# Moving 72 edge-row scatters from the first convolution into the recurrent blocks of a fused graph network

## The chip, the cores and the metric

One core of a Trainium2 chip runs the whole program. The metric is the time of one execution on the device in microseconds; smaller is better. The core has TensorE (matmuls; PE in the profile), VectorE (DVE), ScalarE (ACT), GpSimd (POOL) and SyncE (SP), which here only issues DMAs. "PEq" or "SPq" in a row is the instruction queue of that engine.

## The reference

Four graph networks follow one another on 3125 nodes of 128 features, with 100,000 edges (padded to 782 columns of 128 edges), each followed by a residual sum and a normalisation:

```python
x = _layernorm(x + _L0_gnn_ref(...))   # two convolutions: h = x + segment_sum(x[src], dst); two dense layers
x = _layernorm(x + _L1_gnn_ref(...))   # two attention layers
x = _layernorm(x + _L2_gnn_ref(...))   # four recurrent blocks: neighbour sum, dense, gates
x = _layernorm(x + _L3_gnn_ref(x, edge_attr_64, src, dst, ...))
# the last: W = silu(edge_attr @ W1 + b1) @ W2 + b2; msgs = h[dst] * W; sum of msgs by src; two dense layers
```

The last network sums its messages by source node, while the edges arrive ordered by destination. Its input rows, one of 66 floats for each edge (64 attributes and the two node numbers), must therefore be brought into another order.

## The kernel before

The nodes are padded to 3200 and held as 25 tiles of 128. Sums over neighbours in the two convolutions (`gin_conv`, tags g0 and g1) and the recurrent blocks (`gru_block`) are dense matmuls with a 3200 x 3200 matrix of edge counts: `sum_neighbours` (L370) runs 25 tiles times 3 bf16 parts of the features for each half of a group of 5 tiles (GT), and 5 groups (NG) make a layer.

The program is a chain of blocks, each with one program for each engine, and each ends in a barrier of all engines; what runs on two engines in one block is joined there. The order is: constants, `edge_order` (computes the slot of every edge in the new order), `build_counts`, `gin_conv` g0 (the first convolution) and g1, `edge_tables`, two `attention` layers, `softmax_norm`, four times `gru_block`, `edge_messages`, `node_update`.

The edge rows reach their new order by scatters that GpSimd issues beside other work. One scatter writes 128 rows of 264 bytes from SBUF to the table `sorted` in device memory, at the slots that `edge_order` found. There are 782 of them, one for each column of edges, and only `edge_messages` reads `sorted`. The class `Sender` (L1722) does them in batches: `begin` loads the slots of its share and the rows of the first batch; `send` waits for the batch's rows, copies its slots to an index tile (L1749), issues the scatters one by one (L1756), and halfway issues the load of the next batch's rows into the other of two buffers (L1737), after the scatters that read that buffer are done; `end` waits until all scatters have landed. Its core:

```python
        for u in range(self.size):
            if u == self.size // 2:
                if not first:
                    pool.wait_ge(self.sent[1 - s], j * full + s * full)
                self.load(pool, n + 1, 1 - s)
            pool.indirect_dma_start(out=self.D["sorted"], in_=self.held[s][:, u, :], in_offset=None,
                                    out_offset=...).then_inc(self.sent[s], 16)
```

How many go where is set by constants (L1593 to L1596), each a triple of first column, scatters in a batch and number of batches: 168 in `build_counts`, 150 in the first convolution, 32 in `edge_tables`, 108 in each of the four recurrent blocks. In `gin_conv` and `gru_block` GpSimd does nothing else. SyncE loads the features, in g0 also writes the count matrix to memory for the recurrent blocks (L439, 20 MB), and stores each group's result (L446, L1487). In `gin_conv` a group goes from the sums (L370) over a copy by VectorE (L504) and two dense layers (L463, L471) with ScalarE (L483) to VectorE (L510, L514) and the store; in `gru_block` over two dense layers (L1504, L1508), the gates on ScalarE and VectorE, five transposes (L1512) and copies (L1572) to the store. The rows named L420 and L1469 are the places where those blocks are opened and closed.

Of the kernel before, what the change touches and what calls it, by code (L numbers as in the profile page):

```python
# [14 lines left out]
NT = -(-N_NODES // P)  # L15
# [524 lines left out]
def edge_tables(nc, K, D):  # L540
# [5 lines left out]
    with ExitStack() as ctx:  # L546
# [19 lines left out]
        bound = m.sb("p_bound", [1, NT + 1])  # L566
        sender = Sender(m, D, "p", *TABLE_SENDS)
        boundi = m.sb("p_boundi", [1, NT + 1], I32)
# [873 lines left out]
def gru_block(nc, K, D, AT, b, source, from_scale, to_scale, parts, target, residual):  # L1442

    with ExitStack() as ctx:
# [11 lines left out]
        split = Split(m, source, 1, parts, [work[:, i, :].rearrange("p (t c) -> p t c", c=P) for i in range(3)], from_scale)  # L1456
        sender = Sender(m, D, "r", *GRU_SENDS[b])
        y = m.sb("r_y", [P, GT, P])
# [132 lines left out]
NEAR_STEPS = 4  # L1591
ROWW = RBF + 2
COUNT_SENDS = (0, 7, NT - 1)  # L1593
GIN_SENDS = (7 * (NT - 1), 15, 10)
TABLE_SENDS = (7 * (NT - 1) + 150, 16, 2)
GRU_SENDS = [(7 * (NT - 1) + 182 + 108 * b, 9, 12) for b in range(4)]  # L1596
NSC = 7 * (NT - 1) + 182 + 432
SROWS = (NGRP + 1) * EGRP
FILL = (NGRP + 1) * SUB // 11
# [445 lines left out]
def gnn_program(nc, D):  # L2045
# [27 lines left out]
    with ExitStack() as ctx:  # L2073
# [6 lines left out]
        with ExitStack() as ctx2:  # L2080
            AT = Mem(nc, ctx2).sb("gin_counts", [P, NT, NP], BF16)
            build_counts(nc, K, D, AT)
            gin_conv(nc, K, D, AT, "g0", D["x"], 1, D["L0_W1a"], D["L0_b1a"], D["L0_W2a"], D["L0_b2a"], 2 * P,
                     D["gin1"], None, sends=GIN_SENDS, keep=D["kept"])
            gin_conv(nc, K, D, AT, "g1", D["gin1"], 2, D["L0_W1b"], D["L0_b1b"], D["L0_W2b"], D["L0_b2b"], P,
# [95 lines left out]
```

## Time and profile before

| | |
|---|---|
| median of 3 runs | 6274.49 us |
| lowest and highest | 6272.12, 6283.94 us |
| span of the profiled execution | 6282.4 us |
| TensorE busy, share of the span | 4259.3 us, 68% |
| VectorE | 3797.3 us, 60% |
| GpSimd | 3528.6 us, 56% |
| first convolution, start to start of the next block | 966.8 to 1227.4 us |
| four recurrent blocks | 4365.2 to 5093.1 us |

Times in a row are in microseconds from the start of the span. Only one execution is profiled, and its rows are exact for that one alone. A stage that ends in a barrier is as long as its slowest engine, whatever the shares of the span say; so one looks for what each engine waited for at the stage's end. A wait at a barrier is put down to the queue that released it, which is the one that passes the barrier on and not always the one that was late.

### The profile page before, as it was taken

The numbers are of one execution on the slowest core, as the hardware profiler recorded it, in microseconds if no ns is written. First come the engines' busy times: TensorE is split into PE (matmuls) and PEld (weight loads), VectorE is DVE, ScalarE is ACT, GpSimd is POOL, SyncE is SP. The second block draws the span as 40 slices with busy tenths as digits, with TensorE's granted clock in tenths as the row PEclk, the third lists the DMA queues.
The fourth block names the chain that finished last, engine by engine and source line by source line (L and its number), as shares of the span: only waits on it lengthen the run. The fifth ranks groups of instructions, "written<-read, shape, count | busy, mean of one in ns | idle before, by whom it ended". The sixth has DMA issues, their size and how long they took to land. (4 is left out here: it accounts for less than half of the span.)

```text
span 6282.4 us, 102133 instructions
## 1 busy us (share of the span) xinstructions
PE 4259.3 (68%) x26578; PEld 2971.7 (47%) x26579; DVE 3797.3 (60%) x8630; ACT 1047.3 (17%) x1871; POOL 3528.6 (56%) x3626
## 2 busy tenths in 40 slices
PE   3666667395267777776256666666787777788884
PEld 1111115263156565655245555554454555566663
DVE  8777772154589999998456666666211235555553
ACT  0111111102211111111211111111211222222221
POOL 1222224502377777774277777771666667777771
PEclk9999999697589999998567777777898888988885
DMA  4000004201244444442333233334212222222233
GB/s 197 15 12 15 15 12 187 70 15 36 71 128 119 124 118 125 117 126 79 129 82 81 75 82 81 81 76 155 60 55 63 70 71 78 78 78 77 78 78 40
DMA packets 331742, 510.88 MB, mean 81 GB/s; under 512 B 104053, under 2 KB 245407, under 8 KB 321686
## 3 DMA queue, kind: packets, MB, share of 16 engines
q0 software_dynamic: 129376, 287.12, 17.6%
q1 hardware_dynamic: 202166, 221.78, 10.9%
q14 instruction: 158, 1.29, 0.1%
q8 instruction: 42, 0.69, 0.0%
HBM read 406.76 MB, written 101.86 MB: 81 GB/s over the span
## 5 line engine op out<-in xcount | busy, mean ns | idle before, releaser
L1061 POOL DMA_INDIRECT e_ring<-att_rows,e_near x1760 | 1791.3, 1018 | 553.7 <-issue 473.8
L1130 PE MATMUL e_psum<-e_ring,e_whole_pick 128*128 128x264 f32 (+1 forms) x3520 | 840.6, 392 | 244.5 <-DVE e_ring L1295 238.7
L1839 POOL DMA_INDIRECT e_nodes<-x,e_edges x832 | 808.6, 972 | 266.3 <-issue 239.2
L1130 PEld LDWEIGHTS e_psum<-e_ring,e_whole_pick 128*128 128x128 f32 x3520 | 643.6, 227 | 369.5 <-issue 175.8
L1085 PE MATMUL e_px<-t_parts,e_pick 128*128 x5280 | 671.9, 268 | 102.0 <-DVE e_pick L1193 51.5
L1209 DVE TENSOR_TENSOR e_prod<-e_px,e_ring 128x512 f32<-128x512 f32 x660 | 449.9, 682 | 386.8 <-DMA e_ring<-att_rows,e_near 277.4
L285 PE MATMUL b_acc<-b_pick_key,b_pick_lo 128*128 128x416 bf16 (+1 forms) x1960 | 495.9, 341 | 169.9 <-DVE b_pick_key L256 151.6
L1756 POOL DMA_INDIRECT sorted<-rx_held,rx_index x432 | 425.1, 984 | 220.4 <-issue 209.4
L1085 PEld LDWEIGHTS e_px<-t_parts,e_pick 128*128 128x128 bf16 x5280 | 442.8, 107 | 188.7 <-issue 119.2
L1173 ACT ACTIVATE e_whole_pick<-e_pturn 128x512 f32<-128x512 bf16 x440 | 261.7, 595 | 1351.6 <-PE e_pturn L1121 1329.0
L256 DVE TENSOR_SCALAR b_pick_key<-b_lane,b_base,b_keyf 128x800 bf16<-128x800 int16 x980 | 477.1, 487 | 0.0
L1199 DVE TENSOR_REDUCE e_dots<-e_prod 128x8 f32<-128x512 f32 (+1 forms) x660 | 444.8, 674 | 0.0
L1295 DVE TENSOR_TENSOR e_ring<-e_ring 128x1024 f32<-128x1024 f32 (+1 forms) x440 | 416.1, 946 | 26.7 <-issue 26.7
L1876 PE MATMUL e_pa<-e_msg,e_pick 128*128 128x128 f32 x1672 | 296.4, 332 | 191.5 <-DVEq L1938 191.2
L1876 PEld LDWEIGHTS e_pa<-e_msg,e_pick 128*128 128x128 f32 x1672 | 248.6, 228 | 362.7 <-DVEq L1938 355.2
L255 DVE TENSOR_SCALAR b_pick_lo<-b_lane,b_lof 128x128 bf16<-128x128 int16 x980 | 255.7, 261 | 236.8 <-PE b_acc L285 192.7
L370 PE MATMUL g_pa<-gin_counts,g_parts 128*128 x2250 | 312.7, 302 | 120.4 <-DMA g_b<-in_L_b2b 101.9
L285 PEld LDWEIGHTS b_acc<-b_pick_key,b_pick_lo 128*128 128x128 bf16 x1960 | 120.2, 97 | 529.9 <-DVE b_pick_key L256 514.9
L1946 DVE TENSOR_TENSOR agg<-agg,e_pa 128x128 f32 x418 | 120.5, 288 | 381.6 <-PE e_pa L1876 234.5
L209 POOL TENSOR_TENSOR gin_counts<-gin_counts,identb 128x128 bf16 (+1 forms) x25 | 12.7, 507 | 568.9 <-ACT gin_counts L266 568.9
L1089 PE MATMUL e_pside<-t_side,e_pick 128*128 x1760 | 332.1, 189 | 0.0
L370 PEld LDWEIGHTS g_pa<-gin_counts,g_parts 128*128 128x128 bf16 x2250 | 221.1, 99 | 211.9 <-issue 123.5
(348 smaller groups left out, 6766.7 us busy)
## 6 DMA issues: line engine op xcount, KB each, us to landing
e_relb<-place SPq DMA_DIRECT2D x56, 1024.0 KB, 6.0
e_ring<-att_rows,e_near POOLq DMA_INDIRECT x1760, 2.6
sorted<-o_fill SPq DMA_DIRECT2D x11, 2508.0 KB
e_edges<-sorted SPq DMA_DIRECT2D x209, 132.0 KB
kept<-gin_counts SPq DMA_DIRECT2D x5, 4000.0 KB
rx_held<-in_edge_rows POOLq DMA_DIRECT2D x52, 297.0 KB
e_nodes<-x,e_edges POOLq DMA_INDIRECT x832
gru_late<-kept SPq DMA_DIRECT2D x3, 4000.0 KB, 32.6
```

Of the source, the lines that this page charges most:

```text
L256: dve.tensor_scalar(pick_key[:, b, :], lane[:, :], base[:, ds(w, 1)], keyf[:, ds(c, 1)], ALU.add, ALU.is_equal).then_inc(picked, 1)
L285: mm = pe.matmul(acc[q % 2][:, h, 0:z - a], pick_lo[:, b, :], pick_key[:, b, a:z], start=False, stop=False, skip_group_check=True)
L370: mm = pe.matmul(banks, parts[:, k, j, f * P:(f + 1) * P], AT[:, j, ds(g * GW + half * HW, HW)], start=(j == 0 and k == 0), stop=(j == NT ...
L1061: pool.indirect_dma_start(out=ring[:, s, r, 0:wd + HEADS], out_offset=None, in_=xrows, in_offset=bass.IndirectOffsetOnAxis(ap=near[:, s, r ...
L1085: mm = pe.matmul(px[g % 2][:, x * wd:(x + 1) * wd], pick[:, 1 - s, r, :], parts[:, n, ds(t, 1), :].rearrange("p o c -> p (o c)"), start=(n ...
L1130: mm = pe.matmul(psum[q % 2][:, 0:RING], whole_pick[:, q % 2, c, :], ring[:, s, q * G + c, :], start=(c == 0), stop=(c == G - 1))
L1199: dve.tensor_reduce(dots[:, s, :, g * XB:(g + 1) * XB].rearrange("p h x -> p x h"), prod[:, g % 4, :].rearrange("p (x h c) -> p x h c", x= ...
L1209: dve.tensor_tensor(prod[:, g % 4, :].rearrange("p (x c) -> p x c", x=XB), px[g % 2][:, :].rearrange("p (x c) -> p x c", x=XB), ring[:, 1 ...
L1295: dve.tensor_tensor(rows_, rows_, ring[:, s, q * G:(q + 1) * G, wd:wd + HEADS].unsqueeze(3).broadcast_to([P, G, HEADS, ch]), ALU.mult).the ...
L1756: pool.indirect_dma_start(out=self.D["sorted"], in_=self.held[s][:, u, :], in_offset=None, out_offset=bass.IndirectOffsetOnAxis(ap=self.in ...
L1839: pool.indirect_dma_start(out=nodes[:, q, u, :], out_offset=None, in_=source, in_offset=bass.IndirectOffsetOnAxis(ap=edges[:, q, u, RBF + ...
L1876: mm = pe.matmul(pa[s][:, part * P:(part + 1) * P], pick[:, s, u, :], msg[:, s, u, :], start=(u % (SUB // HALVES) == 0), stop=(u % (SUB // ...
```

## The change

Only the constants that divide the scatters change. The first convolution issues 6 batches of 13, 78 in all, instead of 10 of 15. The edge tables keep their 2 batches of 16 and take the columns that follow. Each of the four recurrent blocks issues 14 batches of 9, 126 in all, instead of 12 of 9. The same 782 columns are scattered, each once.

```diff
 COUNT_SENDS = (0, 7, NT - 1)
-GIN_SENDS = (7 * (NT - 1), 15, 10)
-TABLE_SENDS = (7 * (NT - 1) + 150, 16, 2)
-GRU_SENDS = [(7 * (NT - 1) + 182 + 108 * b, 9, 12) for b in range(4)]
+GIN_SENDS = (7 * (NT - 1), 13, 6)
+TABLE_SENDS = (7 * (NT - 1) + 78, 16, 2)
+GRU_SENDS = [(7 * (NT - 1) + 110 + 126 * b, 9, 14) for b in range(4)]
```

## Rows read from the trace of the kernel before

**Rows 1.** The page: span and count of instructions.
```profile
span 6282.4 us, 102133 instructions
```

**Rows 2.** First convolution: busy us of PE, PEld, DVE, ACT, POOL; PEclk, DMA share, GB/s.
```profile
967.00:1227.00 260.00, 141.91 (x890) 100.82 (x890) 27.84 (x50) 19.59 (x35) 156.11 (x172) 0.79 0.39 141
```

**Rows 3.** SyncE's waits, 970 to 1240: who for whom, total us, times, longest.
```profile
SPq L420 <- PEq L420: 87.3, 1, 87.3
...
SPq L420 <- DMA gin<-g_y: 2.7, 1, 2.7
```

**Rows 4.** Timeline, end of first convolution: start, us, engine, line, operation, idle before.
```profile
1135.57 0.38 SPq L446 DMA_DIRECT2D gin<-g_y  x1
...
1222.33 0.96 POOL L1756 DMA_INDIRECT sorted<-g0x_held,g0x_index  x1 [0.30 <-issue]
1227.42 0.96 SPq L314 DMA_DIRECT2D g_hid<-gin  x2
```

**Rows 5.** SyncE's waits at the end of recurrent blocks 0, 1, 2 and 3.
```profile
SPq L1469 <- PEq L1469: 5.0, 1, 5.0
...
SPq L1469 <- PEq L1469: 4.9, 1, 4.9
...
SPq L1469 <- PEq L1469: 6.6, 1, 6.6
...
SPq L1469 <- PEq L1469: 2.2, 1, 2.2
```

**Rows 6.** SyncE's wait at the end of the second convolution.
```profile
SPq L420 <- PEq L420: 0.2, 1, 0.2
```

**Rows 7.** Timeline, end of recurrent block 0.
```profile
4536.48 0.38 SPq L1487 DMA_DIRECT2D state<-r_y  x1
...
4541.40 0.95 POOL L1756 DMA_INDIRECT sorted<-rx_held,rx_index  x1 [0.30 <-issue]
4545.97 1.52 SPq L314 DMA_DIRECT2D r_work<-state  x3
```

**Rows 8.** Timeline, GpSimd, first convolution: first scatter of batches 2 to 5 and 10.
```profile
1026.04 0.98 POOL L1756 DMA_INDIRECT sorted<-g0x_held,g0x_index  x1 [19.09 <-issue]
...
1049.11 0.98 POOL L1756 DMA_INDIRECT sorted<-g0x_held,g0x_index  x1 [3.24 <-issue]
...
1071.03 0.98 POOL L1756 DMA_INDIRECT sorted<-g0x_held,g0x_index  x1 [2.47 <-issue]
...
1093.44 0.98 POOL L1756 DMA_INDIRECT sorted<-g0x_held,g0x_index  x1 [2.48 <-issue]
...
1204.02 0.98 POOL L1756 DMA_INDIRECT sorted<-g0x_held,g0x_index  x1 [2.48 <-issue]
```

**Rows 9.** First convolution, two shorter stretches, columns as in Rows 2.
```profile
1006.00:1026.00 20.00, 19.39 (x120) 14.21 (x120) 3.44 (x7) 0.00 (x0) 0.20 (x1) 0.91 1.00 418
1026.00:1040.00 14.00, 11.55 (x69) 8.19 (x67) 1.30 (x3) 1.78 (x4) 10.91 (x12) 1.00 0.68 251
```

**Rows 10.** Timeline, GpSimd, recurrent block 0: first scatter of batches 2, 5, 6, 12.
```profile
4388.97 0.97 POOL L1756 DMA_INDIRECT sorted<-rx_held,rx_index  x1 [2.23 <-issue]
...
4431.45 0.98 POOL L1756 DMA_INDIRECT sorted<-rx_held,rx_index  x1 [2.22 <-issue]
...
4445.56 0.98 POOL L1756 DMA_INDIRECT sorted<-rx_held,rx_index  x1 [2.23 <-issue]
...
4530.67 0.98 POOL L1756 DMA_INDIRECT sorted<-rx_held,rx_index  x1 [2.42 <-issue]
```

**Rows 11.** Between recurrent blocks 0 and 1, columns as in Rows 2 (PEclk third last).
```profile
4540.00:4546.00 6.00, 0.00 (x0) 0.00 (x0) 0.00 (x0) 0.00 (x0) 1.91 (x2) 0.50 0.05 17
...
4556.00:4560.00 4.00, 4.00 (x18) 2.34 (x17) 3.26 (x5) 3.08 (x5) 3.27 (x3) 0.55 0.65 182
```

**Rows 12.** Recurrent block 0: its first scatter; its 108 scatters by line (busy, mean ns).
```profile
4372.85 1.46 POOL L1756 DMA_INDIRECT sorted<-rx_held,rx_index  x1 [1.02 <-issue]
...
L1756 POOL DMA_INDIRECT sorted<-rx_held,rx_index x108 | 106.2, 983 | 55.1 <-issue 52.4 <-DMA rx_held<-in_edge_rows 2.7
```

## Prediction

> **What bounds the kernel now.** I read the page for the span [rows 1], then the busy time of the first convolution by stretch [rows 2], and then SyncE's waits, because every stage ends in a barrier of all engines, and the queue that issues the last store shows how long it stood there. In the first convolution TensorE is busy 142 us of 260 and GpSimd 156: neither is full, so the shares decide nothing. SyncE's waits do [rows 3]: after its last store had landed (2.7 us) it stood 87.3 us at the block's end. The wait is put down to PEq, since that queue passes the barrier on; the timeline names who was late [rows 4]. The last store is issued at 1135.57, GpSimd's last scatter at 1222.33, and the second convolution begins at 1227.42, 5.1 us behind the scatter. So 87 us of this stage are scatters with nothing beside them.
>
> The same view of the four recurrent blocks [rows 5] shows 5.0, 4.9, 6.6 and 2.2 us. The second convolution, which has no scatters, waits 0.2 us at that place [rows 6]; that is the barrier itself. The recurrent blocks too end on GpSimd, then, by 4.8, 4.7, 6.4 and 2.0 us. The timeline of block 0 agrees [rows 7]: last store at 4536.48, last scatter at 4541.40, next block at 4545.97, 4.6 us behind it. On this reading the forecast hangs: the first convolution has no room for its 150 scatters, and the recurrent blocks have none left either.
>
> **The change, part by part.** No scatter is added or dropped: 150 + 4 x 108 = 582 before, 78 + 4 x 126 = 582 after. The 32 of the edge tables only take other columns, with the same count, sizes and code: 0.
>
> The first convolution goes from 10 batches of 15 to 6 of 13. Its compute side is untouched: SyncE is free at 1135.57 + 0.38 + 2.7 = 1138.65, and without the late GpSimd the next stage begins at 1227.42 - 87.3 + 0.2 = 1140.3. Is GpSimd done by then? Its second batch starts only at 1026.04, after 19.1 us without a releaser [rows 8], just when the DMA engines, until then 1.00 busy at 418 GB/s, come down to 0.68 [rows 9]; SyncE's copy of the count matrix to memory (20 MB) is what fills them. That copy stays, so I keep 1026.04. The following batches start 23.07, 21.92 and 22.41 us apart [rows 8]. The last one has 15 scatters in 1222.33 - 1204.02 = 18.31 us, that is 14 steps of 1.26 us and 0.6 for the load halfway. Two scatters fewer make the periods 20.55, 19.40 and then 19.89 us, and the last 12 x 1.26 + 0.6 = 15.8. Last scatter: 1026.04 + 20.55 + 19.40 + 2 x 19.89 + 15.8 = 1121.6; with the 5.1 us behind it, 1126.7. Compute ends the stage, with 13.6 us to spare, and the stage loses 87.3 - 0.2 = **87.1 us**. Bounds 81.6 (the stall comes twice, C below) and 90 (the clock, below).
>
> Each recurrent block gets two more batches of 9. A batch takes 4445.56 - 4431.45 = 14.11 us, and ten of them from 4388.97 to 4530.67 take 14.17 each [rows 10]. They queue behind the work GpSimd already has, and GpSimd is what ends the block, so nothing covers them: 28.2 us a block. Who waits: all other engines at the barrier, and the next block, which reads the stored state, is late by all of it. Each batch's load of rows is issued half a batch ahead and is inside the 14.11; the slot table's load grows from 108 to 126 columns beside the first load of rows, 0. Four blocks: 8 x 14.12 = **113.0 us**, bounds 112.8 and 114.5 (8 x 14.11 and, rounded up, the longer mean with a late one among them). The room that the blocks have, 4.8 + 4.7 + 6.4 + 2.0 = 17.9 us, lies on the compute side, where no scatter can use it.
>
> TensorE's clock: it stands between the two convolutions for some 100 us now and for some 15 us after the change. Between blocks 0 and 1, a pause of 20 us, the granted clock is at 0.50 (1.2 GHz), and in the 4 us after TensorE has started again at 0.55 [rows 11]. 15 us is near to 20, so I take the same slow start as now, 0; if the clock held, the first 6 us of matmuls would take half, 3 us of gain at most. In the recurrent blocks TensorE gets 28 us more to spare, and its clock changes nothing.
>
> Scatters beside VectorE's work: the first of block 0 takes 1.46 us, the mean of its 108 is 0.983 [rows 12], and late ones take 0.96 [rows 7]. The moved 18 become the last of each block and run after VectorE has handed over its last result (4536.48 in block 0). I take 0. The other end is D.
>
> **The sum.** -87.1 + 113.0 = +25.9 us. Against the profiled execution 6282.4 + 25.9 = 6308.3 us of span. That span lies 7.9 us over the median of the runs, 6274.5, and inside their spread (6272.1 to 6283.9), so nothing large lies around it; I carry the difference over to the median: **6300.4 us**, 0.41% slower.
>
> **The rivals.**
> A. The change wins. The mechanism: GpSimd is not what holds the end of the recurrent blocks, and the extra batches slide under something else that ends some 5 us after the store. It decides from 21.8 us a block (87.1 / 4): were 7.5 of the 28.2 us hidden in each, the sum would be 4 x 20.7 - 87.1 = -4.3, and with 11 us hidden -18.3, 6256. For it speaks only that the profile names PEq. Against it: 4.6 us from the last scatter to the next block in block 0, where it is 5.1 in the first convolution, in which GpSimd is alone beyond doubt. 3%.
> B. It does little: of each block's 28.2 us some 4 to 6 are hidden (the 5 us of A, without more), or the executions, which differ by 12 us as they are, swallow half of the difference. Sum +6, 6280 to 6287. What speaks against it is as in A. 7%. Within 0.2% means within 12.5 us, about what a measurement of this kernel can tell from no change.
> C. The first convolution still ends on GpSimd. If the stall of 19.1 us comes a second time, the last scatter goes to 1140.7, and the next stage begins at 1145.8 instead of 1140.3: 5.5 us given back, 6305.9. For it: batches of 13 change what stands in the queue. Against it: the DMA engines are down to 0.68 after 1026 [rows 9]. 7%.
> D. The moved scatters stretch, because VectorE's work delays GpSimd. Where all 72 took 1.46 instead of 0.96 us [rows 12], that would be 36 us more, 6336. Against it: VectorE has no work left when they run. 3%.
> The Trainium skill speaks on the side of D: by "SBUF — State Buffer", section "SBUF: two separate sides", a DMA issued from GpSimd cannot have its descriptors written while VectorE holds their shared port pair. The long first scatters fit it, the late ones show no trace of it.
>
> The forecast itself has 80%. The bounds give +22.8 (112.8 - 90) to +32.9 (114.5 - 81.6), and a few us of the executions' spread come on either side: 6292 to 6309. The range, 6288 to 6312, takes in C with it, and leaves out A, B and D.
> Chances: faster 0.03, same 0.07, slower 0.90.
>
> **What the profile after would show.** Right, if SyncE's wait at L420 in the first convolution falls from 87.3 to about 0.2 us and the second convolution begins near 1140; if its waits at L1469 rise to about 33, 33, 35 and 30 us and the four blocks together, 727.9 us now, take 841; if the first convolution's last scatter stands near 1122; and if the mean scatter stays at 0.98 us. Wrong, if a block grows by clearly less than 28 us (A, B), if L420 still waits some us (C), if late scatters take more than 0.96 us (D), or if the second convolution changes by more than 3 us, for which I have no term.

## The result

The changed kernel takes 6302.5 us (median of 6 runs, 6295.6 to 6305.1), the kernel before 6281.3 us (6 runs, 6272.1 to 6285.4; the three runs shown ahead of the prediction are among them). The ratio is 1.0034, with a 95% interval from 1.0023 to 1.0046: 21 us slower, 14 to 29. The forecast was 6300.4 us and +25.9 us.

The page of the changed kernel: span, and busy time of each engine.

```profile
span 6300.2 us, 102169 instructions
...
PE 4235.4 (67%) x26578; PEld 2950.7 (47%) x26579; DVE 3795.9 (60%) x8630; ACT 1047.9 (17%) x1871; POOL 3528.0 (56%) x3634
```

No work was added: TensorE and VectorE run as many instructions as before, and GpSimd has 8 more, the index copies and loads of four more batches on balance. TensorE's busy time is 24 us less (4259.3 before); 15 us of that lie in the edge messages and what follows, whose code is the same and whose mean granted clock was 0.84 there instead of 0.82. What changed is where the other engines stand still. The end of the first convolution, in SyncE's waits (who for whom, total us, times, longest) and in the timeline, which answers to [rows 3, 4]:

```profile
SPq L420 <- DMA gin<-g_y: 2.7, 1, 2.7
...
SPq L420 <- PEq L420: 0.2, 1, 0.2
```

```profile
1115.44 0.95 POOL L1756 DMA_INDIRECT sorted<-g0x_held,g0x_index  x1 [0.30 <-issue]
...
1134.19 0.38 SPq L446 DMA_DIRECT2D gin<-g_y  x1
1138.95 0.96 SPq L314 DMA_DIRECT2D g_hid<-gin  x2
```

The last scatter now stands 19 us ahead of the last store, and the wait of 87.3 us is 0.2. The ends of the four recurrent blocks, SyncE's waits again, against [rows 5]:

```profile
SPq L1469 <- PEq L1469: 33.1, 1, 33.1
...
SPq L1469 <- PEq L1469: 33.1, 1, 33.1
...
SPq L1469 <- PEq L1469: 34.9, 1, 34.9
...
SPq L1469 <- PEq L1469: 27.9, 1, 27.9
```

The waits of 5.0, 4.9, 6.6 and 2.2 us have become 33.1, 33.1, 34.9 and 27.9. In the timeline, the first loads of blocks 0 to 3 and of the stage behind them; their distances are the lengths of the blocks:

```profile
4267.63 1.54 SPq L314 DMA_DIRECT2D r_work<-x  x3
...
4477.55 1.52 SPq L314 DMA_DIRECT2D r_work<-state  x3
...
4687.95 1.53 SPq L314 DMA_DIRECT2D r_work<-state  x3
...
4898.72 1.53 SPq L314 DMA_DIRECT2D r_work<-state  x3
...
5109.89 0.57 SPq L1810 DMA_DIRECT2D e_w<-in_e_W  x1
```

By such first loads, the stages of the two profiled executions are (the differences are of unrounded values):

| stage | before, us | after, us | difference |
|---|---|---|---|
| all before the first convolution | 966.8 | 966.2 | -0.5 |
| first convolution | 260.7 | 172.7 | -87.9 |
| second convolution | 275.2 | 272.2 | -3.0 |
| edge tables | 73.4 | 73.5 | +0.2 |
| attention and softmax_norm | 2789.3 | 2782.9 | -6.3 |
| recurrent blocks 0 to 3 | 180.8, 181.8, 182.5, 182.8 | 209.9, 210.4, 210.8, 211.2 | +114.4 |
| edge messages to the end | 1189.4 | 1190.3 | +1.0 |

The first convolution and the blocks give +26.5 us, where +25.9 were forecast. The spans differ by only 17.8: the stages whose code is the same were some 9 us shorter in the execution after. Of these, 5 us are the second attention stage, and they are not the change's: it took 1284.8 us before and 1279.7 after, and between 1279.0 and 1285.2 in the other kernels below, whether their first convolution was short or long. The 3.0 us of the second convolution are taken up under the clock.

### The profile page after: what moved, and what is told of

The parts are those of the page before. It is cut to its first block and busy times, and to the rows that moved or that the text cites. A ratio compares the mean times of both kernels' runs of the same rounds, so it can differ in the third digit from the quotient of the medians.

```text
span 6300.2 us, 102169 instructions
## 1 busy us (share of the span) xinstructions
PE 4235.4 (67%) x26578; PEld 2950.7 (47%) x26579; DVE 3795.9 (60%) x8630; ACT 1047.9 (17%) x1871; POOL 3528.0 (56%) x3634
## 5 line engine op out<-in xcount | busy, mean ns | idle before, releaser
L1085 PE MATMUL e_px<-t_parts,e_pick 128*128 x5280 | 671.4, 268 | 100.6 <-DVE e_pick L1193 50.9
L1756 POOL DMA_INDIRECT sorted<-rx_held,rx_index x504 | 494.7, 981 | 258.4 <-issue 245.0
L1295 DVE TENSOR_TENSOR e_ring<-e_ring 128x1024 f32<-128x1024 f32 (+1 forms) x440 | 416.0, 946 | 26.5 <-issue 26.5
L1876 PE MATMUL e_pa<-e_msg,e_pick 128*128 128x128 f32 x1672 | 277.5, 317 | 206.3 <-DVEq L1938 206.2
L1876 PEld LDWEIGHTS e_pa<-e_msg,e_pick 128*128 128x128 f32 x1672 | 231.3, 214 | 378.8 <-DVEq L1938 374.1
L370 PE MATMUL r_pa<-gru_early,gru_parts 128*128 x1200 | 213.1, 347 | 180.7 <-DMA r_bh<-in_gru_bh 115.1
L370 PE MATMUL g_pa<-gin_counts,g_parts 128*128 x2250 | 311.3, 301 | 32.5 <-DMA g_b<-in_L_b2b 14.3
```

What stands on the lines that cost most here:

```text
L370: mm = pe.matmul(banks, parts[:, k, j, f * P:(f + 1) * P], AT[:, j, ds(g * GW + half * HW, HW)], start=(j == 0 and k == 0), stop=(j == NT ...
L1085: mm = pe.matmul(px[g % 2][:, x * wd:(x + 1) * wd], pick[:, 1 - s, r, :], parts[:, n, ds(t, 1), :].rearrange("p o c -> p (o c)"), start=(n ...
L1295: dve.tensor_tensor(rows_, rows_, ring[:, s, q * G:(q + 1) * G, wd:wd + HEADS].unsqueeze(3).broadcast_to([P, G, HEADS, ch]), ALU.mult).the ...
L1876: mm = pe.matmul(pa[s][:, part * P:(part + 1) * P], pick[:, s, u, :], msg[:, s, u, :], start=(u % (SUB // HALVES) == 0), stop=(u % (SUB // ...
```

## The experiments

All are edits of the kernel before, and differences are against its runs on the same chip. A difference with an interval behind it is worked out from the ratio; the plain difference of the medians lies up to 4 us beside it. Lines left out of a diff are marked with `...`; where it shows only `+` lines for a constant, they take the place of the old ones.

**Each half alone.** The first takes 72 scatters out of the first convolution and puts them nowhere:

```diff
-GIN_SENDS = (7 * (NT - 1), 15, 10)
+GIN_SENDS = (7 * (NT - 1), 13, 6)
```

> One half of the change alone: the first convolution issues 78 scatters (6 batches of 13), and everything else is as before; 72 columns of edge rows are left out, so the rows of `sorted` for them stay blank. Theory (each stage is as long as the later of its compute side and its scatters): the whole gain of the changed kernel's first convolution and nothing else, 87.9 us less than before (its stage went from 260.7 to 172.7 us), SyncE's wait at L420 at 0.2 us; about 6193. Rival (the stage's gain is partly an effect on later stages, the attention being 6 us shorter in the profile after): 94 us less and the attention again shorter by 6.

Measured: 6191.7 us against 6281.7, ratio 0.9854 (0.9837 to 0.9870), 92 us less (82 to 102). The first convolution took 173.0 us and its wait at L420 is 0.2 us; the second attention stage took 1285.2 us, as before (1284.8). So the whole gain is the first convolution's, and the rival falls.

The second keeps the 150 scatters and has the blocks do 126:

```diff
-GRU_SENDS = [(7 * (NT - 1) + 182 + 108 * b, 9, 12) for b in range(4)]
+GRU_SENDS = [(7 * (NT - 1) + 110 + 126 * b, 9, 14) for b in range(4)]
```

> The other half alone: each recurrent block issues 126 scatters (14 batches of 9), while the first convolution keeps its 150; 72 columns are scattered twice, to the same slots with the same rows. Theory: nothing covers the extra batches, 8 x 14.12 = 113 us more than before, about 6394, and the four blocks at 210 us each. Rival A of the prediction (something other than GpSimd holds the blocks' end, part of each 28 us is hidden): 87 us or less.

Measured: 6395.0 us, ratio 1.0181 (1.0164 to 1.0198), 113 us more (103 to 124). The ends of its blocks, SyncE's waits:

```profile
SPq L1469 <- PEq L1469: 32.6, 1, 32.6
...
SPq L1469 <- PEq L1469: 33.0, 1, 33.0
...
SPq L1469 <- PEq L1469: 33.1, 1, 33.1
...
SPq L1469 <- PEq L1469: 31.3, 1, 31.3
```

Its four blocks together took 840.2 us, 112.4 more than the 727.8 of before; 8 x 14.12 is 113.0. Nothing of the extra batches was hidden, which rival A needed. By plain medians the two halves are -90.0 and +113.3, which add up to +23.3 us, and the change measured +21.2.

**Fewer scatters in the blocks.** The same lever the other way:

```diff
-GRU_SENDS = [(7 * (NT - 1) + 182 + 108 * b, 9, 12) for b in range(4)]
+GRU_SENDS = [(7 * (NT - 1) + 182 + 108 * b, 9, 10) for b in range(4)]
```

> Two batches fewer in each recurrent block (10 of 9, 90 scatters), all else as before; 72 columns of edge rows are left out. Theory: a block gives back only what it waits for GpSimd, 4.8, 4.7, 6.4 and 2.0 us, then its compute side ends it: 17.9 us less than before, about 6263, and SyncE's waits at L1469 at 0.2 us. Rival (a batch costs 14.1 us of time wherever it stands, for instance by slowing the other engines): 113 us less.

Measured: 6257.5 us, ratio 0.9965 (0.9951 to 0.9979), 22 us less (13 to 31), where 17.9 were expected and the rival said 113. SyncE's waits at L1469 are 0.2 us in all four blocks. The timeline at its blocks' first loads:

```profile
4355.35 1.56 SPq L314 DMA_DIRECT2D r_work<-x  x3
4530.67 1.53 SPq L314 DMA_DIRECT2D r_work<-state  x3
4707.91 1.53 SPq L314 DMA_DIRECT2D r_work<-state  x3
4883.66 1.53 SPq L314 DMA_DIRECT2D r_work<-state  x3
5065.38 0.57 SPq L1810 DMA_DIRECT2D e_w<-in_e_W  x1
```

The blocks took 175.3, 177.2, 175.8 and 181.7 us: 5.4, 4.6, 6.8 and 1.1 less than before, 17.8 in all, where the waits in [rows 5] had promised 4.8, 4.7, 6.4 and 2.0, 17.9 in all. A block that loses two batches of 14 us becomes only 1 to 7 us shorter, and a block that gains two becomes 28 us longer: the curve has its bend just under the 108 scatters of before.

**Another home for the same 72.** The second convolution gets a Sender of its own; the rest of the change's first half stays:

```diff
+GIN_SENDS = (7 * (NT - 1), 13, 6)
+GIN2_SENDS = (7 * (NT - 1) + 78, 2, 36)
+TABLE_SENDS = (7 * (NT - 1) + 150, 16, 2)
...
-                     D["x1"], D["x"], outdeg=outdeg)
+                     D["x1"], D["x"], outdeg=outdeg, sends=GIN2_SENDS)
```

> The same 72 scatters leave the first convolution (78 stay) but go to the second one, whose GpSimd is idle for all of its 272 us; the recurrent blocks keep 108. Buffers there have room for two columns only, so it is 36 batches of 2. Theory: where the compute side is longer, scatters cost nothing; a batch of 2 takes some 5 to 6.5 us (2 x 1.26, 2.5 behind the index copy, 0.9 for the load, and perhaps a wait for the rows), 36 of them 180 to 235 us, hidden: 87 us less than before, about 6194, faster than both kernels. Rival (so small a batch exposes the load, 8 us a batch): 288 us of scatters, the second convolution 20 us longer, 67 us less. Rival (the scatters' transfers slow the convolution's own): its compute side itself grows by more than 3 us.

Measured: 6192.7 us, ratio 0.9857 (0.9841 to 0.9874), 90 us less (79 to 100). The same kernel ran once more on another chip, beside the last version of this section ("the one above"), of which this was expected:

> The version with 72 scatters in the second convolution once more, on the same chip as the one above, so that the two can be compared: 87 to 90 us less than before, 12 to 20 us more than the combined short version.

Measured: 6193.2 us, ratio 0.9861 (0.9844 to 0.9877). The second convolution of the first of the two: GpSimd's last scatters in the timeline (a line of code was added, so that L1756 is now L1757), and SyncE's wait at the end.

```profile
1326.00 0.98 POOL L1757 DMA_INDIRECT sorted<-g1x_held,g1x_index  x1 [1.51 <-DMA sorted<-g1x_held,g1x_index]
...
1330.98 0.98 POOL L1757 DMA_INDIRECT sorted<-g1x_held,g1x_index  x1 [1.58 <-issue]
...
1332.84 0.99 POOL L1757 DMA_INDIRECT sorted<-g1x_held,g1x_index  x1 [0.30 <-issue]
```

```profile
SPq L420 <- PEq L420: 0.2, 1, 0.2
```

A batch of 2 takes 1330.98 - 1326.00 = 4.98 us there, 2.5 us for each scatter where the blocks pay 1.57, and costs nothing: the last one is issued at 1332.8, the stage ends at 1413.1, and it took 272.8 us, against 272.2 in the changed kernel, where it has no scatters. The same 72 scatters that cost 113 us in the blocks are free here.

**What a batch and the stall cost.** The next two took up the two terms of the first convolution that were carried over without proof: what a batch costs of its own, and the 19.1 us ahead of the second batch.

```diff
-GIN_SENDS = (7 * (NT - 1), 15, 10)
+GIN_SENDS = (7 * (NT - 1), 25, 6)
```

> Nothing is moved: the first convolution keeps its 150 scatters, as 6 batches of 25 instead of 10 of 15; all else as before. Theory (a batch costs 1.26 us for each scatter and about 3.4 us of its own, and the stall of the second batch ends when the copy of the count matrix does, at 1021 to 1026, however many scatters stand ahead of it): the ten more scatters of the first batch fall into the stall, and four batches fewer save 4 x 3.4, so the last scatter is at 1026 + 4 x 35.1 + 30.9 = 1197 instead of 1222: 25 us less than before, about 6256. Rival (the stall is the software queue's own and grows with the scatters in it): the saving is the gaps alone, 12 to 14 us.

Measured: 6268.2 us (10 runs) against 6279.4 (19), ratio 0.9985 (0.9975 to 0.9994), 9 us less (4 to 16), not 25. The first convolution took 252.0 us instead of 260.7. Its timeline, index copy and first scatter of the second batch, then the first scatters of the third and the sixth:

```profile
1023.98 0.21 POOL L1749 COPY g0x_index<-g0x_slot 128x25 int32 x1 [14.51 <-DMA g0x_held<-in_edge_rows]
1039.44 0.98 POOL L1756 DMA_INDIRECT sorted<-g0x_held,g0x_index  x1 [15.25 <-issue]
...
1074.49 1.06 POOL L1756 DMA_INDIRECT sorted<-g0x_held,g0x_index  x1 [2.94 <-issue]
...
1181.22 0.98 POOL L1756 DMA_INDIRECT sorted<-g0x_held,g0x_index  x1 [2.92 <-issue]
```

The periods are as worked out (1074.49 - 1039.44 = 35.05), so the gaps of four batches were won. But the ten more scatters of the first batch did not slip into the stall: the second batch starts at 1039.44, 13.4 us behind the 1026.04 of before, which is more than the 12.6 us that the ten take. That is nearer the rival, which had the gaps alone.

The other run moves the copy:

```diff
-                     D["gin1"], None, sends=GIN_SENDS, keep=D["kept"])
+                     D["gin1"], None, sends=GIN_SENDS)
...
-                     D["x1"], D["x"], outdeg=outdeg)
+                     D["x1"], D["x"], outdeg=outdeg, keep=D["kept"])
```

> The copy of the count matrix to memory (20 MB) is issued in the second convolution instead of the first; scatters as before. Theory (it is this copy that holds the first convolution's second batch back): the second batch starts 22.4 us after the first, near 999 instead of 1026, the stage is 27 us shorter, the second convolution unchanged since it doesn't wait for memory after its start: 27 us less, about 6255. Rival (the stall belongs to the queue of indirect DMAs): the batch still starts near 1026, no change. Rival (the copy delays the second convolution's loads): the gain is given back there in part, up to 20 us.

Measured: 6282.1 us (10 runs) against 6279.4 (19), ratio 1.0004 (0.9994 to 1.0013), no change. Inside, the theory and the last rival came true at once. In the first convolution the second batch:

```profile
994.96 0.21 POOL L1749 COPY g0x_index<-g0x_slot 128x15 int32 x1
997.65 0.98 POOL L1756 DMA_INDIRECT sorted<-g0x_held,g0x_index  x1 [2.48 <-issue]
```

starts at 997.65 without a stall, and the stage took 232.1 us, 28.6 less. The second convolution took 302.2, 27.0 more, where the theory had said unchanged and the rival up to 20. Its timeline shows why:

```profile
1220.45 4.75 SPq L439 DMA_DIRECT2D kept<-gin_counts  x5
1228.17 0.41 SPq L444 DMA_DIRECT2D g_y<-in_x  x1
1272.85 0.82 DVE L500 TENSOR_TENSOR g_y<-g_y,g_b 128x640 f32<-128x640 f32 x1 [28.84 <-DMA g_y<-in_x]
```

The load of the residual is issued right behind the copy on the same queue, and VectorE can use it only 45 us after its issue, having waited 28.84 us for it; the sums' way on waits with it. So the copy causes the stall in the first convolution, and in the one other place that was tried it cost as much.

**What the stall waits for.** The rows of the stall name no releaser, but the trace holds more. Between the index copy and a batch's first scatter stands a `pool.drain()` (L1750), which the code ahead of the prediction leaves out. It has a record of its own (shortest, median and longest ns, then its start): here in the first convolution of the kernel before and in the one with batches of 25, and then the packets that each queue moved from 1014 to 1018 us in the kernel before (packets, MB, share of the engines; q1 is SyncE's queue, q0 GpSimd's).

```profile
L1750 POOLq DRAIN  x1: 18550/18550/18550, 1006.7 to 1006.7; - x1
...
L1750 POOLq DRAIN  x1: 14724/14724/14724, 1024.0 to 1024.0; - x1
...
q1 hardware_dynamic: 50, 1.60, 95.8%
q0 software_dynamic: 52, 0.05, 3.8%
```

While the copy runs, the two queues move packets in about equal number. But the copy's are of 32,000 bytes, while of GpSimd's half have 2112 bytes, 16 of them for each scatter, and half have 4. In these 4 us 25 of the scatters' packets were moved, which makes some 2.6 us for each scatter where the issue takes 1.26. So the first batch's scatters, though issued, land slowly. The drain ends when they have:

| scatters in the batch | their last packet ends | drain ends | next scatter | copy's last packet ends |
|---|---|---|---|---|
| 13 (the changed kernel) | 1017.77 | 1020.12 | 1020.86 | 1031.54 |
| 15 (before) | 1023.11 | 1025.29 | 1026.04 | 1032.87 |
| 23 (the last version below) | 1035.21 | 1037.25 | 1038.00 | 1033.47 |
| 25 | 1036.63 | 1038.70 | 1039.44 | 1034.68 |
| 26 (the next version) | 1037.79 | 1039.95 | 1040.70 | 1035.20 |
| 15, the copy moved away | 995.78 | 996.90 | 997.65 | |

In every row, and at all 67 batches behind a first one in the first convolutions of the eleven traces, the drain ends 1.0 to 2.4 us after the last packet of the scatters issued before it. So the stall is GpSimd waiting for its own earlier scatters, which the copy makes slow; that is why it grows with the batch ahead of it and is gone without the copy. Batches of 13 and 15 get through while the copy runs, those of 23 and more only after its last packet. This is read from the traces alone: no run took the drain out.

**All of it together.** The 614 scatters behind `build_counts`, laid where they fit: 104, 88 (2 a batch), 38 and four times 96. The second convolution is called with its Sender as above.

```diff
+GIN_SENDS = (7 * (NT - 1), 26, 4)
+GIN2_SENDS = (7 * (NT - 1) + 104, 2, 44)
+TABLE_SENDS = (7 * (NT - 1) + 192, 19, 2)
+GRU_SENDS = [(7 * (NT - 1) + 230 + 96 * b, 8, 12) for b in range(4)]
```

> All 582 + 32 scatters where they fit under the compute side: 104 in the first convolution (4 batches of 26), 88 in the second (44 of 2, at 5.0 us a batch 221 us of its 272), 38 in the edge tables (2 of 19), 96 in each recurrent block (12 of 8). Theory: every stage ends on its compute side, 87 to 90 us less than before from the convolution and 17.9 to 24 from the blocks: 6170 to 6176, faster than before and than the version with 72 in the second convolution. Rival (the first convolution's 104 scatters don't fit, the stall being longer with 26 of them in the first batch): its stage is up to 10 us longer, 6185. Rival (the tables' 38 scatters pass its compute side): 3 us.

Measured: 6185.1 us, ratio 0.9857 (0.9840 to 0.9873), 90 us less (80 to 100), not 6170 to 6176: the first rival came true. The recurrent blocks lost their waits (0.2 us each), and the tables took their 38 scatters for nothing (73.5 us, 73.4 before), but the first convolution took 186.2 us, and SyncE waited in it for

```profile
SPq L420 <- PEq L420: 11.1, 1, 11.1
```

since its second batch began at 1040.7, 14.7 us later than I had carried over from batches of 15. With that known, 92 scatters go there, and the last block keeps its 108:

```diff
+GIN_SENDS = (7 * (NT - 1), 23, 4)
+GIN2_SENDS = (7 * (NT - 1) + 92, 2, 44)
+TABLE_SENDS = (7 * (NT - 1) + 180, 19, 2)
+GRU_SENDS = [(7 * (NT - 1) + 218 + 96 * b, *((9, 12) if b == 3 else (8, 12))) for b in range(4)]
```

> As the combined version, but with 92 scatters in the first convolution (4 batches of 23) and 108 again in the last recurrent block, which has the least room (it waits 2 us for GpSimd); 88 in the second convolution, 38 in the tables, 96 in each of the other three blocks. Theory: with 23 scatters in the first batch the stall ends near 1037, between the 1020.9 to 1026.0 of 13 and 15 and the 1039.4 to 1040.7 of 25 and 26; then two periods of 23 x 1.26 + 3.4 = 32.5 us and 28.4 for the last batch, last scatter at 1130, free at 1135.5, before the compute side at 1140: the stage is 173 us instead of the 186 of the combined version. All in all 88 us less than before from the convolution and 15.9 to 20 from three blocks: 6171 to 6176. Rival (the stall ends later than 1041 after all): the stage ends on GpSimd again, by as much as it is later.

Measured: 6176.3 us (6171.4 to 6178.4) against 6280.6, ratio 0.9831 (0.9815 to 0.9847), 106 us less (95 to 116), where 6171 to 6176 were expected; the version with 72 in the second convolution took 6193.2 on the same chip. Its first convolution:

```profile
1038.00 0.98 POOL L1757 DMA_INDIRECT sorted<-g0x_held,g0x_index  x1 [14.88 <-issue]
...
1070.81 0.98 POOL L1757 DMA_INDIRECT sorted<-g0x_held,g0x_index  x1 [2.80 <-issue]
...
1103.36 1.04 POOL L1757 DMA_INDIRECT sorted<-g0x_held,g0x_index  x1 [2.78 <-issue]
```

with periods of 32.8 and 32.6 us, a stage of 173.7 us and a wait at L420 of 0.2 us. It is faster than both kernels.

## Why the prediction was right

**The number** is nearer than it should be. 6300.4 us were forecast and 6302.5 measured, but the difference was 21.2 (14 to 29) instead of 25.9, and the base was 6281.3 us over six runs instead of the 6274.5 of three: 6.8 us too low and 4.7 too much cancel, which is luck. The difference by itself lies inside its interval.

**The reading of the barriers** held: the wait that SyncE shows at a stage's end is what the stage would give back. 87.3 us in the first convolution became 87.9 us of gain, and the waits of the blocks, 17.9 us in all, became 17.8 when they lost batches. It holds as far as the compute side repeats itself: block 3's wait rose by 25.7 us only, to 27.9 where about 30 were forecast, while the block grew by 28.4, since its last store was issued 178.8 us into the block instead of 176.1.

**The first convolution's term**, -87.1, measured -87.9 in the profile and -90 (medians) for that half alone. The stage ends on its compute side, as said. The working for GpSimd was too late by 6 us: last scatter at 1115.4, not 1121.6. Its failing step is the second batch's start, which I carried over as 1026.04 because the DMA engines seemed to come down then [rows 9]. They do not, even in the kernel before: the 0.68 is a mean over 14 us, and its first two are still full (columns as in [rows 2]).

```profile
1026.00:1028.00 2.00, 2.00 (x17) 1.43 (x15) 0.00 (x0) 0.00 (x0) 1.66 (x2) 1.00 1.00 432
```

In the changed kernel the second batch starts here:

```profile
1020.86 0.98 POOL L1756 DMA_INDIRECT sorted<-g0x_held,g0x_index  x1 [17.52 <-issue]
```

and the stretch behind it is full as well:

```profile
1021.00:1028.00 7.00, 7.00 (x54) 5.06 (x52) 0.49 (x1) 0.00 (x0) 5.48 (x6) 1.00 1.01 425
```

So the scatters go on some 7 us before the copy is done in the kernel before, and 11 in the changed one. The step to put in its place is that the second batch waits for the scatters of the first, and comes earlier when they are fewer. It cost the forecast nothing because 13.6 us of room stood behind it; the kernel with 104 scatters, built on the same step, missed its time by it. C, a second stall, did not come: the third batch starts 19.3 us after the second.

**The blocks' term**, +113.0, measured +114.4 in the profile and +113.3 (medians) for that half alone. Two batches cost 28.2 us, and the blocks grew by 29.2, 28.6, 28.3 and 28.4. The working named GpSimd as what ends them and left nothing to hide the batches; A and B fall with the run that does the blocks' half alone, and the one with 90 scatters a block shows the bend that they would have needed, on the other side of 108.

**Scatters beside VectorE.** The mean of a scatter stayed: 0.979, 0.988, 0.975 and 0.984 us in blocks 0 to 3, against 0.983 in [rows 12], and the last 18 of a block took 0.96 each, before and after. The moved ones are like the last but two of block 0,

```profile
4470.45 0.96 POOL L1756 DMA_INDIRECT sorted<-rx_held,rx_index  x1 [0.30 <-DMA sorted<-rx_held,rx_index]
```

which runs 30 us after VectorE's last result. D falls for these. The rule of the Trainium skill ("SBUF — State Buffer", section "SBUF: two separate sides") is not refuted by that, since VectorE was idle. What a block's first scatters show in the kernel before is this:

```profile
4374.60 1.29 POOL L1756 DMA_INDIRECT sorted<-rx_held,rx_index  x1 [0.30 <-issue]
4374.95 0.82 DVE L341 TENSOR_TENSOR r_work<-r_work,gru_parts 128x640 f32<-128x640 f32 x1
...
4383.81 4.15 DVE L1546 RECIPROCAL to_scale<-to_scale  x1 [0.32 <-issue]
```

Of the 432 scatters of its four blocks, 47 overlap one of VectorE's TENSOR_TENSORs or SCALAR_TENSOR_TENSORs of some 0.8 us; they took 1.16 us on average, and all 23 above 1.1 us are among them. The other 385 took 0.96, none more than 1.04. Two that lie wholly beside the RECIPROCAL of 4.15 us took 0.95 and 0.96. So what D fears exists, 0.2 us for a scatter beside such an operation, but the moved scatters have none beside them; and length alone does not stretch a scatter. Which property of the operation does was not tried.

**The clock.** The second convolution now starts after a pause of 14.3 us for TensorE. Granted clock (third from the end), in the changed kernel:

```profile
1138.00:1146.00 8.00, 0.00 (x0) 0.00 (x0) 2.11 (x3) 2.52 (x4) 0.00 (x0) 0.50 0.68 181
1148.00:1152.00 4.00, 4.00 (x20) 2.40 (x19) 2.40 (x4) 3.62 (x5) 0.00 (x0) 0.60 0.50 149
1152.00:1156.00 4.00, 4.00 (x32) 2.90 (x30) 3.03 (x4) 3.44 (x5) 0.00 (x0) 1.00 0.55 161
```

It had fallen to 0.50 (1.2 GHz), as after the 102 us of before, and was back at 1.00 4.3 us after TensorE had started again, 6.0 before; the term of 0 holds within these 2 us. The stage's first group took 64.8 to 65.5 us in the six executions with a pause of 14 to 26 us and 65.1 to 66.3 in the four with one of 92 to 102 us and the copy in its old place: about half a microsecond on average. In the two executions of the table it is 1.3 of the 3.0 us (66.1 and 64.8). The other 1.6 are another of the five groups, which took 52.5 us instead of 50.9 in the kernel before. One group was longer like that in four of the five executions with a pause of 74 us or more, and in none of the six with a short one. Why was not looked into, so whether the change has a part in these 1.6 us stays open; the prediction had set 3 us as the mark from which a term would be missing.

**Why the sum is positive** can be said more shortly than I did. With its share of the batch's own cost, a scatter takes 22.4 / 15 = 1.49 us in the first convolution and 14.12 / 9 = 1.57 us in a block. All 72 are paid at 1.57, 113 us. At 1.49 they would have earned 107.5, but only the first 58 or so did, 87.1 us; the others were taken out of a stage that no longer waited for them. That overshoot is some 20 of the 26 us, the smaller batch 5 to 6.

## What to carry to other kernels

Filler work that runs beside a stage is free exactly up to what the stage's other engines leave, and then costs its full length. Before moving it, read the wait at the barrier of both stages: the wait where it leaves is the most that can be won, and where it goes there must be a gap of the other sign, on the queue that would do it. Here both kinds of stage in the move already ended on such work, so the move could only exchange one microsecond for another and, past the bend, only lose, while the stage between, which had none, took it for nothing, even at 2.5 us a scatter instead of 1.6. And a busy share over a stretch is a mean: before a time is hung on it, read the stretch in shorter pieces, and look for the queue's own records (here the drain) where a row names no releaser.

## What the runs showed of the hardware

In the first convolution, a drain of GpSimd (L1750) behind scatters that it had issued ended 1.0 to 2.4 us after their last packet, at each of 67 batches in eleven traces.

Beside a copy of 20 MB issued by SyncE (418 GB/s in the kernel before) the packets of the two queues came in about equal number, whatever their size (50 and 52 in 4 us, 1.60 and 0.05 MB). So 15 scatters, the last issued at 995.7 us, had their last packet at 1023.1; without the copy, the last issued at 994.0, at 995.8. The gap between an index copy and the next scatter, 2.5 us without the copy, was 12.3 to 19.6 us with it over the ten kernels that have it there, and it ended later with more scatters in the batch ahead.

A load issued behind that copy on SyncE's own queue could be used only 45 us after its issue.

A scatter of 128 rows of 264 bytes took 0.96 us, and 1.16 us on average beside a two-tensor operation of VectorE of some 0.8 us (47 of the 432 in the recurrent blocks of the kernel before).
